# A wait that ties the first gathers of a graph-attention pass to the matmuls that use them

## Chip, cores and metric

One core of a Trainium2 chip runs the whole program. The metric is the device time of one execution in microseconds, and the median of several runs is compared. TensorE is PE in the rows, VectorE is DVE, ScalarE is ACT, GpSimd is POOL and SyncE is SP. Each is an instruction queue of its own, and they meet only at semaphores.

## What is computed

A small graph network on 3125 nodes of 256 features and 50000 edges, sorted by their target node:

```python
h   = relu(concat([x, segment_sum(edge_weight * x[dst], src)]) @ W + b)   # first layer
x   = layernorm(x + h)
y   = x
for Wl, Wr, att, b in two_layers:              # GATv2, 8 heads of 32 features, with self loops
    xl, xr = y @ Wl, y @ Wr
    e      = leaky_relu(xl[src] + xr[dst], 0.2)
    score  = sum(e * att, per head)
    alpha  = softmax of score over the edges of one dst
    y      = y + gelu(segment_sum(alpha * xl[src], dst) + b)
x   = layernorm(x + y)
```

The change lies in the loop over the edges of a GATv2 layer. It is built twice, once for each layer; these are called pass one and pass two here.

## The kernel before

The edges lie in blocks of 128, one edge to a partition, and G = 4 blocks make a group. A pass has NG = 110 groups, and K / G = 4 groups (WG) make a chunk. For each group q the following happens.

- **Gather** (POOL, L1058): four indirect DMAs fetch the rows of the edges' source nodes from a table in device memory (`gather_table`, 264 floats a row) into the ring `gath`. The ring holds RING = 12 groups. Each DMA is an instruction on POOL, which writes the descriptors, and lands some us later; `gathered[q % 12]` tells of it.
- **Expand** (PE, L1077 and L1081): four matmuls copy the gathered rows into PSUM, four more add the rows of the target nodes, picked by the one-hot matrix `OHT` that ACT makes (L1260, L1264). The trace shows eight and four pieces of them. The last adds one to `expanded`. There are two PSUM buffers, so `expand(q)` waits until DVE has read group q - 2.
- **Score** (DVE, L1136 and L1146): the leaky relu times the attention vector, and its sum by head.
- **Chunk** (PE, DVE, ACT): after the scores of four groups the running maximum by target node is found with scans and transposes, and the exponents are taken (ACT L1292, L1293), which adds to `exps`.
- **Weigh**: POOL multiplies half of the gathered rows by their exponents (L1015, `by_pool`), DVE the other half (also L1015, `by_dve`).
- **Sum** (PE, L1108): one-hot matmuls add up the weighted rows by target node (`summed`), and DVE adds the result to the accumulator `node` (L1190). For the first group of a chunk it first multiplies the accumulator by a growth factor (L1197, L1198).

PE works in steps t: `expand(t + 1)`, then what the chunk needs, then the sums of group t - LAG, with LAG = 6. So expansion 7 is followed by the sums of group 0, these by expansion 8, and these by the sums of group 1. POOL has one loop in one queue:

```python
for q in range(NG + RING - 2):
    a = q - RING + 2
    if a >= 0:
        pool.wait_ge(exps, 2 * (a // WG) + 2)
        weigh(pool, a, 0, 2, slots(a, 0, 2)[:, :, D:XW]).then_inc(by_pool, 1)
    if q < NG:
        gather(q)
```

So POOL gathers the groups 0 to 9 without a weighing between them, and from then on weighs group q - 10 and gathers group q. A gather of group 12 or later waits until the sums of the group that held its slot of the ring are done. The gathers of groups 0 to 11 fill the ring and wait for nothing.

Before the passes there are a stage that sorts and prepares, one that scatters weighted rows (POOL L670, with ACT L648 ahead of it), one that sums them and one that makes the table; behind each pass there is a short stage that joins the self loops.

Of the kernel before, what the change touches and what calls it, by code (L numbers as in the profile page):

```python
# [71 lines left out]
def build(nc, x, src, dst, edge_weight, W0, b0, gat, out):  # L72
# [46 lines left out]
    with top:  # L119
# [821 lines left out]
        for layer, (_, _, _, bias) in enumerate(gat):  # L941

            ctx, sem, ps = stage()
            with ctx:
# [27 lines left out]
                def by_head(a):  # L972
# [6 lines left out]
                hot_t, expanded, lin_ready, weighted, scored = (  # L979
                    sem("hot_t"), sem("expanded"), sem("lin_ready"), sem("weighted"), sem("scored"))  # L980
# [28 lines left out]
                def slots(q, g0, g1):  # L1009
                    i = G * (q % RING)  # L1010
                    return ROWS[:, i + g0:i + g1, :]

                def weigh(eng, q, g0, g1, by):
                    R = slots(q, g0, g1)[:, :, 0:D].rearrange("p g (h c) -> p g h c", h=H)
                    return eng.tensor_tensor(R, R, by.unsqueeze(3).broadcast_to([P, g1 - g0, H, C]), ALU.mult)  # L1015

                with nc.Block() as block:
# [32 lines left out]
                    @block.gpsimd  # L1050
                    def _(pool):
                        def gather(q):
                            if q >= RING:
                                pool.wait_ge(summed, 2 * (q - RING + 1))
                            pool.nop(nofuse=True)
                            for g in range(G):
                                i = G * q + g
                                pool.indirect_dma_start(ROWS[:, i % (RING * G), 0:XW], None, tab_d[:, :],  # L1058
                                                        bass.IndirectOffsetOnAxis(SRCI[:, i:i + 1], 0)).then_inc(gathered[q % RING], 16)
# [8 lines that stand above are left out]
# [601 lines left out]
```

## Time and profile before

| | |
|---|---|
| median of 3 runs | 2588.24 us (2587.32 to 2589.81) |
| profiled execution | 2584.12 us, span 2582.3 us |
| mean granted TensorE clock | 0.92 of full |
| busy: PE, DVE, ACT, POOL | 2086.6, 1593.4, 1056.8, 1662.7 us |
| pass one: first gather to last sums | 1033.3 to 1731.3 us |
| pass two: first gather to last sums | 1817.3 to 2514.7 us |

All times of rows are microseconds from the start of the span unless marked ns. A PE clock of 1.00 is the 2.4 GHz level, 0.50 the 1.2 GHz level. A row of a timeline can hold several instructions (its count stands behind the x), and then its duration is from the first one's start to the last one's end. Busy time doesn't count waits, branches and the issue of a DMA by SP.

### The profile page before, as it was taken

To read this page: it belongs to the slowest core of one execution; us is meant where nothing else is said; L and a number is where in the kernel's file an instruction comes from. 1 tells how busy PE (TensorE), PEld (TensorE's weight loads), DVE (VectorE), ACT (ScalarE), POOL (GpSimd) and SP (SyncE) were. 2 spreads that over 40 slices of the span, in tenths; PEclk is the share of its full clock that TensorE was granted. 3 is DMA by queue.
4 is the path that set the end of the run, shared out by engine and by line. 5 is a ranking of instruction groups with operands and counts; after the bars stand their busy time and mean duration, and the time that the engine had idled before them with its cause. 6 is when DMAs were issued, how large, how long until landed. Compare 5 with 4: busy or idle time off the path is not lost. (4 is left out here: it accounts for less than half of the span.)

```text
span 2582.3 us, 31699 instructions
## 1 busy us (share of the span) xinstructions
PE 2086.6 (81%) x7770; PEld 1439.5 (56%) x7770; DVE 1593.4 (62%) x3202; ACT 1056.8 (41%) x2798; POOL 1662.7 (64%) x1810
## 2 busy tenths in 40 slices
PE   0656666665499989799999999969699999999975
PEld 0444444444377765466666666645466666666654
DVE  8312111111266666488888888877488888888876
ACT  0233333333000013355555555544355555555543
POOL 3377777777400004788888888836788888888832
PEclk9776778778799999899999999989899999999987
DMA  3355353434499842544444444431444444444443
GB/s 95 83 123 118 120 117 120 114 119 118 124 267 265 264 126 77 132 113 112 113 126 111 112 113 113 108 65 47 123 110 114 112 115 113 114 111 112 113 78 100
DMA packets 208623, 311.81 MB, mean 121 GB/s; under 512 B 33396, under 2 KB 167542, under 8 KB 208471
## 3 DMA queue, kind: packets, MB, share of 16 engines
q0 software_dynamic: 64512, 171.82, 24.7%
q1 hardware_dynamic: 143799, 138.05, 21.1%
q8 instruction: 61, 1.00, 0.2%
q14 instruction: 91, 0.75, 0.1%
q10 hardware_dynamic: 160, 0.20, 0.0%
HBM read 243.75 MB, written 72.66 MB: 123 GB/s over the span
## 5 line engine op out<-in xcount | busy, mean ns | idle before, releaser
L1058 POOL DMA_INDIRECT gath<-gather_table,SRCI x880 | 849.0, 965 | 242.4 <-issue 210.4
L1108 PE MATMUL p_sums<-gath,OH 128*128 128x272 f32 x1760 | 476.6, 410 | 63.2 <-DVE gath L1015 29.1
L670 POOL DMA_INDIRECT rows_by_src<-gath,node x440 | 436.7, 993 | 139.7 <-issue 115.8
L615 PE MATMUL p_expd<-X,OHT 128*128 x880 | 301.6, 504 | 220.6 <-DVE OHT L581 220.5
L1077 PE MATMUL p_expd<-gath,ident 128*128 128x512 f32 x880 | 427.5, 609 | 31.9 <-DMA gath<-gather_table,SRCI 31.5
L1108 PEld LDWEIGHTS p_sums<-gath,OH 128*128 128x128 f32 x1760 | 323.2, 193 | 189.7 <-issue 86.6
L1081 PE MATMUL p_expd<-node,OHT 128*128 x1760 | 417.6, 380 | 0.0
L1081 PEld LDWEIGHTS p_expd<-node,OHT 128*128 128x128 f32 x1760 | 336.4, 191 | 142.0 <-issue 107.4
L615 PEld LDWEIGHTS p_expd<-X,OHT 128*128 128x128 f32 x880 | 210.6, 250 | 300.9 <-issue 264.1
L1136 DVE SCALAR_TENSOR_TENSOR work<-p_expd,VEC 128x512 f32<-128x512 f32 x440 | 282.2, 682 | 136.8 <-PE p_expd L1081 135.8
L648 ACT ACTIVATE gath<-p_expd,node 128x256 f32<-128x256 f32 x440 | 172.7, 476 | 387.7 <-DVE gath L584 336.8
L584 DVE CAST gath<-SRCI 128x4 f32<-128x4 int32 x110 | 24.1, 219 | 457.5 <-DMA rows_by_src<-gath,node 457.5
L1277 ACT ACTIVATE OH<-iota_row,NLOC 128x128 f32<-128x128 f32 x880 | 277.6, 385 | 6.3 <-PE p_sums L1108 6.2
L1146 DVE TENSOR_REDUCE scores<-work 128x32 f32<-128x1056 f32 x220 | 274.6, 1248 | 5.7
L1015 POOL TENSOR_TENSOR gath<-gath 128x512 f32<-128x512 f32 x220 | 232.2, 1058 | 60.3 <-ACT gath L1293 56.8
L748 PE MATMUL p_sums<-gath,OH 128*128 128x256 f32 x976 | 229.7, 389 | 44.5 <-DVE OH L721 43.4
L1077 PEld LDWEIGHTS p_expd<-gath,ident 128*128 128x128 f32 x880 | 160.0, 192 | 157.5 <-issue 108.2
L1260 ACT ACTIVATE OHT<-LBC,minus_p 128x512 f32<-128x512 bf16 x220 | 157.3, 715 | 209.3 <-PE p_expd L1081 209.3
L748 PEld LDWEIGHTS p_sums<-gath,OH 128*128 128x128 f32 x976 | 180.2, 191 | 94.4 <-DVE OH L721 36.6
L810 POOL TENSOR_TENSOR gath<-gath 128x256 f32<-128x256 f32 x25 | 18.3, 731 | 310.4 <-ACT gath L832 310.4
L1190 DVE TENSOR_TENSOR node<-node,p_sums 128x272 f32 x440 | 187.6, 426 | 17.3 <-PE p_sums L1108 15.9
L1282 ACT ACTIVATE OH<-OH,ones 128x512 f32<-128x512 f32 x220 | 155.6, 707 | 0.5
(282 smaller groups left out, 2163.0 us busy)
## 6 DMA issues: line engine op xcount, KB each, us to landing
gath<-rows_by_src SPq DMA_DIRECT2D x122, 514.0 KB, 4.5
LBC<-local_rows SPq DMA_DIRECT2D x330, 128.0 KB, 3.1
gath<-gather_table,SRCI POOLq DMA_INDIRECT x880, 3.0
rows_by_src<-gath,node POOLq DMA_INDIRECT x440, 3.5
gather_table<-gath SPq DMA_DIRECT2D x50, 132.0 KB, 1.7
node<-gather_table SPq DMA_DIRECT2D x2, 3200.0 KB, 11.9
X<-in_x SPq DMA_DIRECT2D x1, 3072.0 KB
x<-X SPq DMA_DIRECT2D x5, 512.0 KB, 3.0
```

What stands on the lines that cost most here:

```text
L615: ins = pe.matmul(expd[q % 2][:, g // 2, (g % 2) * D:(g % 2 + 1) * D], OHT[:, q % 2, g * P:(g + 1) * P], Xv[:, bass.ds(tiles[g // 2], 1), ...
L670: pool.indirect_dma_start(sup_d[:, :], bass.IndirectOffsetOnAxis(POSI[:, i:i + 1], 0), U[:, q % 4, g, :], None, bounds_check=EP - 1, oob_i ...
L748: ins = pe.matmul(sums[s][:, 0:D], OH[:, s % 2, g, :], U[:, s, g, 0:D], start=(g == 0), stop=(g == G - 1))
L1015: return eng.tensor_tensor(R, R, by.unsqueeze(3).broadcast_to([P, g1 - g0, H, C]), ALU.mult)
L1058: pool.indirect_dma_start(ROWS[:, i % (RING * G), 0:XW], None, tab_d[:, :], bass.IndirectOffsetOnAxis(SRCI[:, i:i + 1], 0)).then_inc(gathe ...
L1077: pe.matmul(expd[q % 2][:, k, :].rearrange("p (g n) -> p g n", g=2), ident[:, :], slots(q, 2 * k, 2 * k + 2)[:, :, 0:D], start=True, stop= ...
L1081: ins = pe.matmul(expd[q % 2][:, g // 2, (g % 2) * D:(g % 2 + 1) * D], OHT[:, q % 2, g * P:(g + 1) * P], TARGET[:, bass.ds(tiles[g // 2], ...
L1108: ins = pe.matmul(sums[k][:, 0:RW], OH[:, a % 2, g, :], slots(a, g, g + 1)[:, 0, :], start=(g % 2 == 0), stop=(g % 2 == 1))
L1136: ins = dve.scalar_tensor_tensor(Tv[:, q % 2, 2 * k:2 * k + 2, :, 0:C].rearrange("p g h c -> p g h c"), expd[q % 2][:, k, :].rearrange("p ...
L1146: dve.tensor_reduce(SC[:, q // WG % 2, :, k:k + G].rearrange("p h k -> p k h"), Tv[:, q % 2], AX, ALU.add).then_inc(scored, 1)
L1190: dve.tensor_tensor(ACC[:, bass.ds(j, 1), :], ACC[:, bass.ds(j, 1), :], sums[k][:, 0:RW].unsqueeze(1), ALU.add).then_inc(added, 1)
L1277: ins = act.activation(OH[:, a % 2, g, :], iota_row[:, :], ACT.Abs, bias=NLOC[:, i:i + 1])
```

## The change

While the ring fills, the gather of group q waits until `expanded` has reached q - 2, that is, until PE has expanded the groups 0 to q - 3. It holds for the groups 3 to 11 of both passes. `expanded` existed before, and ACT, DVE and SP wait for it already.

```diff
 def gather(q):
     if q >= RING:
         pool.wait_ge(summed, 2 * (q - RING + 1))
+    elif q >= 3:
+        pool.wait_ge(expanded, q - 2)
     pool.nop(nofuse=True)
     for g in range(G):
         i = G * q + g
```

## Rows read from the trace of the kernel before

**Rows 1.** The page, costliest groups: busy, mean ns | idle before, releaser

```profile
L1058 POOL DMA_INDIRECT gath<-gather_table,SRCI x880 | 849.0, 965 | 242.4 <-issue 210.4
```

**Rows 2.** Windows: length, busy time by engine, granted PE clock, DMA share, GB/s

```profile
core 0: us, PE busy (x) PEld busy (x) DVE busy (x) ACT busy (x) POOL busy (x), PEclk, DMA share, GB/s
1085.20:1088.60 3.40, 3.40 (x9) 2.19 (x8) 1.47 (x3) 0.00 (x0) 2.49 (x4) 0.50 0.38 107
1867.00:1873.60 6.60, 5.14 (x10) 3.53 (x11) 2.05 (x4) 1.62 (x4) 5.48 (x7) 0.50 0.44 124
...
1108.00:1685.00 577.00, 555.17 (x2112) 373.67 (x2111) 479.67 (x889) 334.72 (x888) 472.34 (x481) 1.00 0.46 113
```

**Rows 3.** Timeline of POOL, pass one: start, duration, instruction, idle before it

```profile
1083.26 1.05 POOL L1015 TENSOR_TENSOR gath<-gath 128x512 f32<-128x512 f32 x1
...
1089.23 1.05 POOL L1015 TENSOR_TENSOR gath<-gath 128x512 f32<-128x512 f32 x1
1090.44 0.98 POOL L1058 DMA_INDIRECT gath<-gather_table,SRCI  x1 [0.16 <-issue]
...
1095.19 1.06 POOL L1015 TENSOR_TENSOR gath<-gath 128x512 f32<-128x512 f32 x1
```

**Rows 4.** Timeline of PE around the first sums, pass one, then pass two

```profile
1074.73 1.99 PE L1081 MATMUL p_expd<-node,OHT 128*128 x8
...
1084.56 3.38 PE L1108 MATMUL p_sums<-gath,OH 128*128 128x272 f32 x8 [4.28 <-POOL gath L1015]
...
1089.88 1.89 PE L1081 MATMUL p_expd<-node,OHT 128*128 x8
...
1097.21 1.08 PE L1108 MATMUL p_sums<-gath,OH 128*128 128x272 f32 x4
...
1858.47 2.65 PE L1081 MATMUL p_expd<-node,OHT 128*128 x8
...
1868.46 3.97 PE L1108 MATMUL p_sums<-gath,OH 128*128 128x272 f32 x8 [3.79 <-POOL gath L1015]
...
1874.65 1.89 PE L1081 MATMUL p_expd<-node,OHT 128*128 x8
```

**Rows 5.** Timeline of POOL, pass two: group 9, group 11, end of gathers

```profile
1862.43 0.95 POOL L1058 DMA_INDIRECT gath<-gather_table,SRCI  x1 [0.30 <-issue]
...
1867.15 1.05 POOL L1015 TENSOR_TENSOR gath<-gath 128x512 f32<-128x512 f32 x1
...
1874.34 0.98 POOL L1058 DMA_INDIRECT gath<-gather_table,SRCI  x1 [0.16 <-issue]
...
2468.43 4.06 POOL L1015 TENSOR_TENSOR gath<-gath 128x512 f32<-128x512 f32 x4
```

**Rows 6.** Timeline of all engines: first scatter, and begin of pass one

```profile
105.33 1.20 ACT L648 ACTIVATE gath<-p_expd,node 128x256 f32<-128x256 f32 x3
...
107.49 1.03 POOL L670 DMA_INDIRECT rows_by_src<-gath,node  x1 [19.35 <-ACT gath L648]
...
1032.56 2.99 SPq L1043 DMA_DIRECT2D LBC<-local_rows  x4
1033.28 1.02 POOL L1058 DMA_INDIRECT gath<-gather_table,SRCI  x1 [2.51 <-POOLq L108]
```

**Rows 7.** Timelines near the end of pass one: POOL and PE

```profile
1673.02 1.06 POOL L1015 TENSOR_TENSOR gath<-gath 128x512 f32<-128x512 f32 x1
...
1674.29 1.16 PE L1108 MATMUL p_sums<-gath,OH 128*128 128x272 f32 x4
...
1684.95 4.05 POOL L1015 TENSOR_TENSOR gath<-gath 128x512 f32<-128x512 f32 x4
1706.49 4.07 POOL L1015 TENSOR_TENSOR gath<-gath 128x512 f32<-128x512 f32 x4 [17.49 <-ACT gath L1293]
```

**Rows 8.** Timelines: DVE's growth factor beside the first gather of a group

```profile
1132.17 0.43 DVE L1197 TENSOR_TENSOR node<-node,grow 128x256 f32 x1 [0.21 <-DVE node L1190]
1132.26 1.20 POOL L1058 DMA_INDIRECT gath<-gather_table,SRCI  x1 [0.16 <-issue]
...
1964.09 1.19 POOL L1058 DMA_INDIRECT gath<-gather_table,SRCI  x1 [0.16 <-issue]
```

## Prediction

> **What bounds the kernel now.** Read the page first, then the two passes alone, since only they hold the changed lines. The costliest group of the page is POOL's indirect gather, 880 instructions of 0.965 us, and nearly all the idle time before them (210.4 of 242.4 us) is "issue", the 0.3 us between two descriptors; it waits for others next to nothing [rows 1]. The windows of pass one say that PE is busy 555.2 of 577 us from 1108 to 1685 at full clock, so by busy share PE looks like the bound [rows 2]. The timeline of POOL decides it. A group costs POOL one weighing (1.05 us) and four gathers, 5.97 us from weighing to weighing (1083.26, 1089.23, then 1095.19 us) [rows 3]. The first weighing of pass one is at 1083.26 and the row that holds the one a hundred groups later starts at 1684.95 us [rows 3, 7]: 601.7 us, against 100 x 5.97 = 597. The other 4.7 us are dealt with below. In pass two it is 2468.43 - 1867.15 = 601.3 us [rows 5]. So POOL never waits between its first gather and its last; it runs on a timetable of its own, and PE follows it. At the end of pass one PE's sums of group 98 start at 1674.29 us, 0.21 us after POOL's weighing of that group ends (1673.02 + 1.06) [rows 7]. A POOL that is late by d there makes PE late by d. PE has little play, yet it has some: it is the follower.
>
> **The change part by part.** Nothing is removed and no data moves elsewhere. Nine waits are added in each of the two passes, ahead of the gathers of groups 3 to 11. Group q waits until PE has expanded group q - 3. From group 12 on the old wait stands as it was.
>
> Groups 3 to 9 come with four gathers at 1.25 us, 5.0 us a group, from 1033.28 us on, so group q starts at about 1033.3 + 5.0q [rows 6]; PE expands them about one group behind. The tightest of these is group 9 of pass two. It starts at 1862.43 us and needs expansion 6, which ends at 1858.47 + 2.65 = 1861.12 us [rows 4, 5]: 1.3 us of play, and more for the others (group 9 of pass one: about 1078.3 by the same count, against an expansion 6 that ends at 1074.73 + 1.99 = 1076.72). Group 10 needs expansion 7, done before PE goes idle for POOL's first weighing. These eight waits find their count reached and cost nothing; what hides them is the gather still running on POOL while its queue reads the wait.
>
> Group 11 is different, because here POOL waits for work that waited for POOL. Expansion 8 stands behind the sums of group 0 in PE's queue, and those wait 4.28 us for POOL's weighing of group 0, which is queued behind the gathers of group 9 [rows 3, 4]. The sums start at 1084.56; after them expansion 8 ends at 1089.88 + 1.89 = 1091.77 us. The gather of group 11 started at 1090.44 us. It is held 1.33 us. In pass two expansion 8 ends at 1874.65 + 1.89 = 1876.54 us and the gather started at 1874.34: 2.20 us [rows 4, 5]. Behind the waiting instruction stand the four gathers of group 11, the weighing of group 2 and all later groups of the same queue.
>
> To this comes the way from the release to the first descriptor, with POOL's pipe empty. No wait of the passes shows it, since none of them holds POOL today. Two places are near. In the scatter stage ACT's fourth scaling ends at 106.53 and the first scatter starts at 107.49 us: 0.97 us. After the barrier at the start of pass one SP's first transfer starts at 1032.56 and POOL's first gather at 1033.28 us: 0.7 us, a lower bound, since SP needs something too [rows 6]. I take 0.9, as the first is the same kind of wait and the same kind of instruction; the bounds are 0.6 and 1.0. The Trainium skill, "Advanced Engine Details and Errata", section Network/Comms, gives 50 to 100 ns for a sequencer to read a semaphore; if that were all, the stall would be 1.33 + 0.1 and 2.20 + 0.1, 3.7 us in total. The row with 0.97 us speaks against it.
>
> The stall is then 1.33 + 0.9 = 2.23 us and 2.20 + 0.9 = 3.10 us, 5.33 us together. The first gather after an empty pipe takes 1.02 us instead of 0.98 [rows 3, 6]: 0.1 us for both passes.
>
> Is it caught up? PE has play right behind the stall: sums of group 2 start at 1097.21 and their weighing ended at 1096.25 us, 0.96 us earlier [rows 3, 4]. But this only means that PE falls into step with POOL some groups sooner. POOL has no idle time in which to win back a microsecond, and the last sums hang on POOL [rows 7]. After 1685 POOL waits 17.49 us for ACT's exponents, which hang on PE, so the drain starts late by the same amount.
>
> One small term is left, the 4.7 us from above. Some first gathers take 1.20 instead of 0.98 us, those that run beside DVE's multiplication of the sums by the growth factor, once in four groups (1132.17 DVE, 1132.26 POOL) [rows 8]. 4.7 / 0.2 is 23 of these in pass one, 4.3 / 0.2 is 21 in pass two. They come from 1132 us on in pass one and regularly from 1964 us on in pass two [rows 8], that is, once PE and DVE are in step with POOL. With the stall they are in step sooner: one more in pass one, two in pass two, 0.6 us. Bounds: none, and five (1.0 us). The Trainium skill, "SBUF — State Buffer", section Terms, says that DVE and GpSimd hold a shared port exclusively and the loser blocks for the whole instruction; by it a gather would lose up to 0.43 us, and these rows show 0.2.
>
> Sum: 5.33 + 0.1 + 0.6 = 6.0 us. The profiled execution of 2584.12 us (span 2582.3) would become 2590.1 (span 2588.3). The median of the runs is 4.1 us above that execution; I carry the difference over, 2588.24 + 6.0 = **2594.2 us**, +0.23%. About 0.2% (5.2 us) is what a measurement of this kernel can tell from no change, so the forecast lies just past that line.
>
> What moves the sum most is PE's clock while it does sums 0 and expansion 8, just after its idle. In pass one 3.4 us of them ran at 0.50 (the level of 1.2 GHz), in pass two 5.1 us, from 1868.46 to 1873.6, of a stretch that began before them [rows 2, 4]. Work at half speed loses half its time: 1.7 and 2.6 us. All at full speed the stalls would be 2.23 - 1.7 = 0.5 and 3.10 - 2.6 = 0.5 us, 1.0 together; with 3.4 us more at half speed in each they would be 8.7. Idle of 4.28 us came before the fall both times, so I expect it again, and take 3.0 to 8.5 us as bounds.
>
> **The rivals.**
> *The same stall, but below the line.* Mechanism as above, with less of the half-speed clock or a release of 0.6 us: 1.9 + 2.8 = 4.7 us, or 3 us with a shorter slow stretch, 2591 to 2593. It is the low half of the forecast, and "no change" by measurement.
> *A second stall at group 9.* Expansion 6 also ran partly at half speed (2.65 instead of 1.89 us for its second half) [rows 4]. With 3.4 us more of that it ends 1.7 us later, and the 1.3 us of play less the 0.9 of the release are used up: 1.3 us of stall in pass two, 0.8 in pass one. All behind it moves too, the weighing of group 0 included, so it adds to the stall of group 11: +7 to +8.5 us, 2596. For it: the play is just 0.4 us net. Against it: both passes of this execution keep it.
> *The wait does nothing.* If POOL's queue had the gathers of group 11 dispatched before the count matters, or if PE's backlog covered it: 2588.2. Against it: the gather of group 11 starts before expansion 8 ends in both passes, and the wait stands ahead of it.
> *Faster.* The 44 long first gathers cost 9 us. A stall that shifts POOL against DVE for good would free them: -9 + 5.4, 2584.7 us. It decides from 27 avoided on (5.4 / 0.2). Against it: both passes began with another distance between PE and POOL and both ended in the same step, so the distance is not kept.
>
> **How the numbers follow.** Stall at group 11 alone, passed on whole: 0.77, of it 0.46 past the line and 0.31 below it. Second stall: 0.12, nearly all past the line. No effect: 0.07. Faster: 0.04, half of it by over 0.2%. Slower by over 0.2%: 0.46 + 0.11 = 0.57. Within: 0.41. Faster: 0.02. The range takes the clock's bounds of 3.0 and 8.5 us and 1 us of scatter between runs (2587.32 to 2589.81): 2590.2 to 2597.8.
>
> **What would show it.** POOL idle once per pass before the first gather of group 11, 2 to 3 us, released by an expansion of PE; no idle before groups 3 to 10; the weighings after it again 5.97 us apart; the last gather of each pass late by the stall; PE waiting for the weighing of group 2. Idle of 0.2 us there would refute the release time; a last gather that is not late would refute that POOL sets the pace; expansion 8 without a half-speed stretch would make the forecast too high.

## The result: slower by 0.29%, and the profile after

| | before | changed |
|---|---|---|
| median of 7 runs | 2587.32 us (2584.63 to 2589.81) | 2594.91 us (2591.12 to 2598.44) |
| profiled execution | 2584.12 us, span 2582.3 | 2591.98 us, span 2590.2 |

The ratio is 1.0029, with a 95% interval of 1.0019 to 1.0038: 5 to 10 us slower. Other chips on which the kernel before takes about 2586 us agree with it as far as they were tried (experiments 1 to 4). Two more chips take 2724 and 2735 us for the kernel before. On the second of them the same change made it faster by 1%, and on the first the waits ahead of groups 3 to 10 alone did; experiment 7 is about that.

POOL's timeline of the changed kernel (start, duration, instruction, idle before it), around group 11 of pass one and of pass two, and at the last gathers of each:

```profile
1088.91 1.06 POOL L1015 TENSOR_TENSOR gath<-gath 128x512 f32<-128x512 f32 x1
1092.93 0.98 POOL L1060 DMA_INDIRECT gath<-gather_table,SRCI  x1 [2.96 <-PE p_expd L1083]
...
1097.70 1.05 POOL L1015 TENSOR_TENSOR gath<-gath 128x512 f32<-128x512 f32 x1
...
1687.89 4.05 POOL L1015 TENSOR_TENSOR gath<-gath 128x512 f32<-128x512 f32 x4
...
1879.29 1.06 POOL L1015 TENSOR_TENSOR gath<-gath 128x512 f32<-128x512 f32 x1
1882.37 0.98 POOL L1060 DMA_INDIRECT gath<-gather_table,SRCI  x1 [2.02 <-PE p_expd L1083]
...
2477.13 2.06 POOL L1015 TENSOR_TENSOR gath<-gath 128x512 f32<-128x512 f32 x2
```

Between the weighing of group 1 and the first gather of group 11 there were 0.16 us of idle [rows 3]; now there are 2.96 and 2.02 us, and PE's expansion ends them. That is 2.80 + 1.86 = 4.66 us more. PE's timeline at the same places:

```profile
1084.25 3.96 PE L1110 MATMUL p_sums<-gath,OH 128*128 128x272 f32 x8 [4.28 <-POOL gath L1015]
...
1090.29 1.89 PE L1083 MATMUL p_expd<-node,OHT 128*128 x8
...
1098.96 2.07 PE L1110 MATMUL p_sums<-gath,OH 128*128 128x272 f32 x8 [1.18 <-issue]
...
1874.63 3.54 PE L1110 MATMUL p_sums<-gath,OH 128*128 128x272 f32 x8 [5.29 <-POOL gath L1015]
...
1879.72 1.89 PE L1083 MATMUL p_expd<-node,OHT 128*128 x8
```

Expansion 8 ends at 1090.29 + 1.89 = 1092.18 us and the gather of group 11 starts at 1092.93: the release takes 0.75 us. In pass two it is 1881.61 to 1882.37, 0.76 us. (In the source an expansion is two matmuls at L1079 and four at L1083; the trace shows them as four and eight pieces.) PE now waits 1.18 us before the sums of group 2 start, 0.21 us after their weighing ends (1097.70 + 1.05 = 1098.75); before, they had 0.96 us of play [rows 3, 4].

The idle of POOL ahead of all 880 gathers of the changed kernel, by what ended it:

```profile
L1060 POOL DMA_INDIRECT gath<-gather_table,SRCI x880: 942/949/1231, 1032.8 to 2476.2; - x176
its engine sat idle before it (us, times) until:
  issue: 208.8, 780
  PE p_sums L1110: 28.7, 94
  PE p_expd L1083: 5.6, 4
  POOLq L108: 4.0, 2
```

The four events by an expansion are the two stalls and two ordinary gaps of 0.3 us behind an early release. From the first gather to the weighing of group 100 it was 1684.95 - 1033.28 = 651.67 us in pass one before [rows 6, 7] and is 1687.89 - 1032.83 = 655.06 now, 3.39 more. In pass two, whose first gather was at 1817.33 us and is at 1823.46, 651.10 became 653.67, 2.57 more. Together 5.96 us. The spans differ by 7.9 us: 3.2 us more lie between the two stretches, and what stands before the first and behind the second is 1.3 us shorter.

### The profile page after: what moved, and what is told of

It reads as the page before. It is cut to its first block and busy times, and to the rows that moved or that the text cites. A ratio compares the mean times of both kernels' runs of the same rounds, so it can differ in the third digit from the quotient of the medians.

```text
span 2590.2 us, 31717 instructions
## 1 busy us (share of the span) xinstructions
PE 2083.3 (80%) x7770; PEld 1438.5 (56%) x7770; DVE 1596.0 (62%) x3202; ACT 1056.7 (41%) x2798; POOL 1663.2 (64%) x1810
## 5 line engine op out<-in xcount | busy, mean ns | idle before, releaser
L1079 PE MATMUL p_expd<-gath,ident 128*128 128x512 f32 x880 | 424.9, 606 | 32.5 <-DMA gath<-gather_table,SRCI 31.9
L1083 PE MATMUL p_expd<-node,OHT 128*128 x1760 | 417.5, 380 | 0.0
L1083 PEld LDWEIGHTS p_expd<-node,OHT 128*128 128x128 f32 x1760 | 336.1, 191 | 141.3 <-issue 106.7
L1079 PEld LDWEIGHTS p_expd<-gath,ident 128*128 128x128 f32 x880 | 159.2, 192 | 157.1 <-issue 107.1
```

Source lines behind the costliest of these rows:

```text
L1079: pe.matmul(expd[q % 2][:, k, :].rearrange("p (g n) -> p g n", g=2), ident[:, :], slots(q, 2 * k, 2 * k + 2)[:, :, 0:D], start=True, stop= ...
L1083: ins = pe.matmul(expd[q % 2][:, g // 2, (g % 2) * D:(g % 2 + 1) * D], OHT[:, q % 2, g * P:(g + 1) * P], TARGET[:, bass.ds(tiles[g // 2], ...
```

## The experiments

Two theories stood at first. **A**: POOL sets the pace of a pass, the wait holds it once in each, and what it is held comes out at the end. **B**: the other eight waits cost something too. Further rivals are named with their run. The runs went to several chips; each is compared with the kernel before on its own chip. All line numbers of the changed kernel are two higher behind the new lines.

**1. Group 11 alone.**

```diff
-    elif q >= 3:
+    elif q == RING - 1:
         pool.wait_ge(expanded, q - 2)
```

> The new wait is kept ahead of the gather of group 11 alone; groups 3 to 10 have none. Theory A (one stall per pass, at group 11, passed on to the end): as with all nine waits, +6 us over the kernel before (+4.5 to +8), POOL idle for 2 to 3 us ahead of group 11 in each pass. Theory B (the eight other waits cost something too, as instructions in POOL's queue or by holding back its reading ahead): clearly less than with all nine, +3 us or below.

2590.91 us against 2584.92, ratio 1.0026 (1.0016 to 1.0035). POOL is idle 2.08 and 2.05 us ahead of group 11. On another chip of the same speed it was run again beside the kernel before itself.

> The wait ahead of group 11 alone. Chip like the first: +6 us over the kernel before, as measured there. Chip like the second, theory E (the gain of 28 us there comes from the waits ahead of groups 4, 8 and 9, which hold POOL's gathers back so that the small loads land): these waits are gone, so the gain is gone, the fill takes 70 us or more again, and the time is 0 to +8 us over the kernel before. Theory F (the gain comes from group 11): most of the 28 us stay.

2594.59 us against 2586.77, ratio 1.0027 (1.0016 to 1.0039), with idle of 2.27 and 3.05 us. One wait of nine makes the whole loss.

> The kernel before itself, for a profile from the same chip as the runs beside it. Ratio 1.000. On a chip like the first (some 2585 us): ring filled to the first weighing in 50 us, 6.02 us a group after it. On a chip like the second (some 2735 us), theory E: ACT's first step of the one-hot matrix waits 20 us or more for its small load in the fill of the ring, since POOL's free-running gathers stand ahead of that load in the DMA engines, and the first weighing comes 70 us or more after the first gather.

Its ratio was 1.000 (0.9989 to 1.0011). In this execution the stretch from first gather to weighing 100 took 652.8 and 652.4 us, against 651.7 and 651.1 in the one shown: about 1 us of a pass is scatter between executions of one kernel.

**2. All but group 11.**

```diff
-    elif q >= 3:
+    elif 3 <= q < RING - 1:
         pool.wait_ge(expanded, q - 2)
```

> The new waits stand ahead of groups 3 to 10, and group 11 has none. Theory A: no change against the kernel before, within 2.5 us, and no idle of POOL above 0.31 us between the gathers of groups 0 to 9. Theory B: +2 us or more.

2584.08 us against 2584.92, ratio 1.0000 (0.9992 to 1.0009), and no idle of POOL above 0.31 us in the fill. Theory B falls.

**3. A longer stall in the same place.**

```diff
-    elif q >= 3:
-        pool.wait_ge(expanded, q - 2)
+    elif q == RING - 1:
+        pool.wait_ge(expanded, q - 1)
```

> Only group 11 waits, and for expansion 9 in place of 8. Expansion 9 ended at 1097.16 and 1881.93 us in the kernel before, the gather of group 11 began at 1090.44 and 1874.34. Theory A, with the 0.76 us that the release took in the changed kernel's trace: stalls of 7.5 and 8.4 us, so +16 us over the kernel before (+14 to +19), and +10 over the change. Theory C (PE has play, and what is lost early is won back over the hundred groups that follow, so a longer stall costs hardly more): +6 to +9 us.

2600.28 us, ratio 1.0064 (1.0050 to 1.0077), so 13 to 20 us, middle 16.5. POOL's timeline at group 11 of pass one and pass two:

```profile
1087.56 1.06 POOL L1015 TENSOR_TENSOR gath<-gath 128x512 f32<-128x512 f32 x1
1096.92 0.98 POOL L1060 DMA_INDIRECT gath<-gather_table,SRCI  x1 [8.29 <-PE p_expd L1083]
...
1888.68 0.98 POOL L1060 DMA_INDIRECT gath<-gather_table,SRCI  x1 [8.40 <-PE p_expd L1083]
```

The idle beyond the usual 0.16 us is 8.13 + 8.24 = 16.4 us, and the loss is as long. Nothing is won back over a hundred groups.

**4. PE kept busy before the first sums.** The change with all its waits, and

```diff
+if t == LAG:
+    for _ in range(4):
+        pe.matmul(sums[1][:, :].rearrange("p (g n) -> p g n", g=2),
+                  ident[:, :], TARGET[:, 0:2, :], start=True, stop=True)
 for a in sums_at(t):
     pe.wait_ge(hots, a + 1)
```

> The change with all its nine waits, and four extra matmuls of 128x512 into the still unused second PSUM buffer of the sums, once a pass, just ahead of the sums of group 0, where PE is idle for some 4 us. They compute nothing that is used. If the half-speed clock on sums 0 and expansion 8 makes most of the stall, expansion 8 now ends 1 to 2 us sooner in each pass, POOL is held 0.6 to 1.5 us in place of 1.9 and 2.8, and the time is +2 to +4 us over the kernel before. If the clock doesn't answer to these matmuls, the stalls stay and the time is that of the change, +6 to +7.

2585.36 us against 2584.92, ratio 1.0006 (0.9998 to 1.0015), so -0.5 to +3.9 us. PE's timeline in pass one, and its windows in both passes (the column behind the busy times is the granted clock):

```profile
1082.35 3.60 PE L1103 MATMUL p_sums<-node,ident 128*128 128x512 f32 x8
1086.79 2.07 PE L1113 MATMUL p_sums<-gath,OH 128*128 128x272 f32 x8 [0.85 <-POOL gath L1015]
1088.70 1.88 PE L1079 MATMUL p_expd<-gath,ident 128*128 128x512 f32 x4
1090.42 1.89 PE L1083 MATMUL p_expd<-node,OHT 128*128 x8
```

```profile
core 0: us, PE busy (x) PEld busy (x) DVE busy (x) ACT busy (x) POOL busy (x), PEclk, DMA share, GB/s
1085.00:1092.00 7.00, 6.15 (x23) 3.83 (x21) 1.83 (x4) 1.46 (x4) 5.88 (x7) 1.00 0.41 119
1870.00:1877.00 7.00, 6.83 (x24) 3.98 (x22) 2.19 (x4) 1.85 (x5) 5.89 (x7) 1.00 0.48 127
```

The same stretches of the changed kernel without the extra matmuls:

```profile
1085.00:1092.00 7.00, 7.00 (x20) 4.72 (x19) 1.47 (x3) 0.00 (x0) 4.04 (x5) 0.71 0.32 87
1874.00:1882.00 8.00, 7.37 (x23) 5.36 (x24) 1.83 (x4) 0.29 (x1) 5.26 (x6) 0.79 0.35 93
```

With the gap filled the clock stayed at 1.00 (2.4 GHz). Without, it was 0.71 and 0.79 on average, that is, partly at 0.50. The sums took 2.07 us in place of 3.96 and 3.54, expansion 8 ended 5.5 us after their start in place of 7.9 and 7.0, and POOL was idle for 0.56 us in each pass, 0.4 more than usual. From the first gather to the weighing of group 100 it was 651.87 and 651.48 us, 0.2 and 0.4 more than in the kernel before. So with all nine waits in place nearly all of the loss of these stretches is gone, more than the expectation had it (+2 to +4 us), and most of the stall is PE at half speed after its own idle. A run with the extra matmuls and no waits is missing.

**5 and 6. POOL made faster.** POOL weighs one block of a group and DVE three, without the new waits and with them.

```diff
-weigh(pool, a, 0, 2, slots(a, 0, 2)[:, :, D:XW])
+weigh(pool, a, 0, 1, slots(a, 0, 1)[:, :, D:XW])
...
-weigh(dve, a, 2, G, ... EXPS[:, G * (a % WG) + 2:G * (a % WG) + G, :])
+weigh(dve, a, 1, G, ... EXPS[:, G * (a % WG) + 1:G * (a % WG) + G, :])
```

The first try came to one of the other chips.

> The kernel before, without the new waits, but POOL weighs one of the four blocks of a group and DVE three, in place of two and two. Theory A (POOL's timetable sets the pace of a pass): a group costs POOL 5.97 - 0.5 = 5.5 us, below the 5.8 us (23.1 us for four groups) that PE needed in pass one before it fell into step, so the pace goes to PE: 6.02 to about 5.8 or 5.9 us a group, 12 to 22 us a pass, 25 to 45 us in all. Theory D (PE or DVE sets the pace, and POOL only seems to): no gain, or a loss, since DVE has 0.3 us more work a group.

> The same division of the weighing with all nine new waits. Theory A: POOL has time in hand once PE sets the pace, so the stall at group 11 (about 2.5 us a pass) costs only what of it reaches PE at the sums of group 2, less than 1 us a pass: 0 to +2.5 us over the kernel with the same division and no waits. The rival, that a stall of POOL costs its length whoever sets the pace: +5 to +6 us.

There they took 3152.56 and 3108.76 us, against 2734.84 for the kernel before: 15% and 14% slower. A group took 8.07 us after the fill, in place of 6.02. Nothing in theory A had foreseen it; what these traces show of the fill is told below. On a chip like the first both were run again.

> No new waits, POOL weighs one block of four and DVE three. Chip like the first, theory A: 12 to 22 us less a pass, 25 to 45 us less in all, as expected before. Theory D: no gain or a loss. Chip like the second: some 3150 us again.

> The same division with the nine waits. Chip like the first: 0 to +2.5 us over the kernel with the same division and no waits (theory A), against +5 to +6 if a stall of POOL costs its length whoever sets the pace. Chip like the second: some 3110 us again, 40 us less than without the waits.

2540.45 us without and 2538.57 us with the waits (four runs each), against 2586.77: ratios 0.9818 (0.9802 to 0.9834) and 0.9810 (0.9793 to 0.9826). The gain of 46 us lies just above the 25 to 45 expected. Windows without the waits, in pass one after the fill:

```profile
1110.00:1630.00 520.00, 508.30 (x1984) 353.16 (x1984) 453.68 (x831) 313.50 (x830) 404.81 (x451) 1.00 0.47 119
```

PE is busy 98% of it, against 96% before [rows 2], and a hundred groups take 576.2 in place of 601.7 us. POOL's queue at group 11 with the waits:

```profile
1091.86 0.63 POOL L1015 TENSOR_TENSOR gath<-gath 128x256 f32<-128x256 f32 x1
1095.16 0.99 POOL L1060 DMA_INDIRECT gath<-gather_table,SRCI  x1 [2.67 <-PE p_expd L1083]
```

The stall is still there, an idle of 2.67 us in pass one and 0.98 us in pass two, and costs nothing that can be measured: from the first gather to the weighing of group 100 it took 626.5 and 624.9 us with the waits and 626.1 in both passes without them. Where POOL doesn't set the pace, its stall is free. This confirms theory A from its other side, and it is the fastest version found: 1.8% below the kernel before on such chips.

**7. The change on another chip.**

> The changed kernel itself, beside the others on one chip: +6 to +8 us over the kernel before (ratio 1.0023 to 1.0031), POOL idle 2 to 3 us ahead of the gather of group 11.

It came to the same chip as the first try of 5 and 6: 2707.26 us against 2734.84, ratio 0.9904 (0.9880 to 0.9929). Faster, against the expectation. That made theory **E**: transfers land later on such a chip, and POOL's gathers, running free in the fill, stand in the way of the small loads of local rows (`LBC`, on SP's queue) that ACT needs to make the one-hot matrices. The early waits hold the gathers back. The rival **F** was that the gain comes from group 11. The last run, on a third chip that takes 2723.71 us for the kernel before, tells them apart.

> The waits ahead of groups 3 to 10 alone, once more, since the calls fall on different chips. Chip like the first: no change against the kernel before, within 2.5 us. Chip like the second (the kernel before at some 2735 us), theory E: these waits hold the whole gain, some 28 us less than the kernel before, first weighing about 60 us after the first gather in each pass; theory F (it comes from group 11): 0 to -5 us.

2696.83 us, ratio 0.9899 (0.9879 to 0.9919), so -27 us with the waits ahead of groups 3 to 10 alone. F falls, as far as two chips can be compared; group 11 alone was not run on such a chip. Nor is there a trace of the kernel before from one: its place is taken by the first try of experiment 5, whose fill up to the first weighing has the same program. ACT's timeline in the fill of pass one, first that kernel without waits, then this last run:

```profile
1144.97 0.72 ACT L1260 ACTIVATE OHT<-LBC,minus_p 128x512 f32<-128x512 bf16 x1 [2.76 <-issue]
...
1161.65 0.72 ACT L1260 ACTIVATE OHT<-LBC,minus_p 128x512 f32<-128x512 bf16 x1 [15.20 <-issue]
...
1188.37 0.72 ACT L1260 ACTIVATE OHT<-LBC,minus_p 128x512 f32<-128x512 bf16 x1 [25.24 <-DMA gather_table<-gath]
```

```profile
1139.69 0.72 ACT L1262 ACTIVATE OHT<-LBC,minus_p 128x512 f32<-128x512 bf16 x1 [2.97 <-issue]
...
1149.58 0.72 ACT L1262 ACTIVATE OHT<-LBC,minus_p 128x512 f32<-128x512 bf16 x1 [8.18 <-PE p_expd L1083]
...
1156.42 0.72 ACT L1262 ACTIVATE OHT<-LBC,minus_p 128x512 f32<-128x512 bf16 x1 [3.39 <-issue]
```

Without waits ACT stands 15.2 and 25.2 us before this one instruction, which needs two things: the load of local rows, and the count `expanded`, which tells that the buffer is free. Theory E says that it is the load. PE's and DVE's timelines of the same kernel say that it is the count:

```profile
1147.34 1.89 PE L1081 MATMUL p_expd<-node,OHT 128*128 x8
...
1151.87 1.89 PE L1081 MATMUL p_expd<-node,OHT 128*128 x8
```

```profile
1144.91 1.29 DVE L1136 SCALAR_TENSOR_TENSOR work<-p_expd,VEC 128x512 f32<-128x512 f32 x2 [11.54 <-issue]
...
1161.59 1.29 DVE L1136 SCALAR_TENSOR_TENSOR work<-p_expd,VEC 128x512 f32<-128x512 f32 x2 [14.10 <-issue]
...
1188.31 1.29 DVE L1136 SCALAR_TENSOR_TENSOR work<-p_expd,VEC 128x512 f32<-128x512 f32 x2 [24.14 <-DMA gather_table<-gath]
```

This step of DVE needs the expansion of its group and no load of local rows. Yet DVE stood until the same moments as ACT, which followed 0.06 us behind it each time. Expansions 1 and 2 ended by PE's rows at 1149.23 and 1153.76 us, so their counts reached both engines 12.4 and 34.6 us late. The load, as far as the trace has it, came long before. SP's queue tells when the loads of groups 3 (the last of the first row) and 4 (the first of the second) were issued:

```profile
1131.88 1.75 SPq L1043 DMA_DIRECT2D LBC<-local_rows  x4
...
1140.88 22.60 SPq L1043 DMA_DIRECT2D LBC<-local_rows  x4
```

A load lands in sixteen parts, and the trace has only some of them: six of group 3, landed from 1136.0 to 1137.3 us, and three of group 4, from 1144.0 to 1144.7, all within 5 us of the issue.

In the run with the waits POOL waits for the same count ahead of group 4. PE's expansion 1, and DVE and POOL:

```profile
1142.40 1.89 PE L1083 MATMUL p_expd<-node,OHT 128*128 x8
```

```profile
1149.52 1.29 DVE L1138 SCALAR_TENSOR_TENSOR work<-p_expd,VEC 128x512 f32<-128x512 f32 x2 [7.32 <-PE p_expd L1083]
```

```profile
1150.24 0.94 POOL L1060 DMA_INDIRECT gath<-gather_table,SRCI  x1 [3.35 <-PE p_expd L1083]
```

Expansion 1 ended at 1144.29 us. ACT, DVE and POOL (less the 0.76 us of its release) all went on at 1149.5, 5.2 us later. The trace records the counts of expansions 1 and 2 at 1149.49 and 1149.62 us, 0.13 apart, though the matmuls of an expansion take 3.7 us. So the signal was late and not the work. Ahead of group 8 it is the same (expansion 5 ended at 1166.04, counted at 1172.74). Group 9 waits for expansion 6, which itself ended late, at 1180.8, behind these. On the chips of 2586 us DVE starts 0.04 us after the end of each of the first five expansions. Theory E is thus wrong in what it says is late.

POOL's first gather and first weighing, the same two kernels:

```profile
1132.61 1.02 POOL L1058 DMA_INDIRECT gath<-gather_table,SRCI  x1 [3.23 <-POOLq L108]
...
1206.85 0.62 POOL L1015 TENSOR_TENSOR gath<-gath 128x256 f32<-128x256 f32 x1 [24.44 <-ACT gath L1293]
```

```profile
1127.06 1.02 POOL L1060 DMA_INDIRECT gath<-gather_table,SRCI  x1 [2.51 <-POOLq L108]
...
1173.48 0.95 POOL L1060 DMA_INDIRECT gath<-gather_table,SRCI  x1 [3.53 <-DMA gather_table<-gath]
...
1181.54 0.95 POOL L1060 DMA_INDIRECT gath<-gather_table,SRCI  x1 [3.29 <-PE p_expd L1083]
...
1186.27 1.06 POOL L1015 TENSOR_TENSOR gath<-gath 128x512 f32<-128x512 f32 x1
```

The fill takes 74.2 us without waits and 59.2 us with them; in pass two 77.2 and 59.5. The first tries of 5 and 6, which differ by the waits alone and ran on one chip, have 74.2 and 77.2 against 59.5 and 59.8: 32 us of the 44 by which their medians differ. On the chips of 2586 us the fill takes 50 us either way.

Why the counts are late is argued and not shown. In the three traces from such chips that have waits, the late counts ahead of groups 4 and 8 came 2.6 to 3.1 us after POOL's last gather before the wait had ended, twelve times of twelve, and elsewhere a gather lands in 3.0 us in the middle. That fits gathers in flight that hold the signal up and let it through once they have landed, so that a held POOL would free it. No run takes the two apart.

The 8.07 us a group of the other division look like the same thing. Once in four groups DVE's scan at L1152 started 3.3 us (in the middle) after the end of the PE transposition it waits for, and the one at L1161 4.6 us after its own; with the same division on a chip of 2586 us it was 0.04 and 0.09 us. Together that is 7.8 us, where four groups took 9.2 us longer. L1161 also needs a load whose landing isn't recorded.

## Why the prediction was right, and where not

**Who sets the pace** was right, and experiments 3 and 5 to 6 show it from both sides: a longer stall costs its whole length, and with a faster POOL a stall costs nothing. By busy share alone PE would have been named.

**Eight free waits** were right where the profile had been taken (experiment 2), and wrong on two chips, where the waits of groups 4, 8 and 9 hold POOL for over 3 us each and, with the others up to group 10, make the gain.

**The stall at group 11** was forecast as 2.23 and 3.10 us and was 2.80 and 1.86; the sum, 5.33 against 4.66, is 0.7 too high. Of it 0.3 us are the release, taken as 0.9 and measured as 0.76. The rest is the end of expansion 8, which hangs on how much of the half-speed stretch falls on it: 2.04 and 1.10 us behind the gather's old place, in place of 1.33 and 2.20. That 5.33 came so near was partly luck: one pass came out 0.6 us over and the other 1.2 under. The 50 to 100 ns of the Trainium skill ("Advanced Engine Details and Errata", Network/Comms) are a part of the 0.76 at most.

**The clock as the largest unknown** was right: without the half-speed stretch the two stalls are 0.4 us each (experiment 4), where the prediction worked out 0.5. The idle before it was 4.28 us in pass one alone and 3.79 in pass two [rows 4], not 4.28 both times.

**The term that failed** is that of the long first gathers. They were to become three more, 0.6 us. Counted by their durations, the changed kernel has 23 and 22 of them, against 23 and 21: one more, 0.2 us. PE and DVE did come into step sooner, but the first long one of pass one still belongs to group 18.

**The second stall at group 9** did not come in any run on a chip like the first. On the two others it did, as a consequence of PE's late signals and not by the clock.

**The sum** of 6.0 us agrees with 5.96 in the profiled execution and with 5 to 10 us over the runs, though partly by luck: the stalls make 4.7, and the 1.3 us left in these stretches are no larger than the scatter between executions. In the runs of experiment 1 the stalls were 3.8 and 5.0 us and the medians 6 to 8 us higher. One to three microseconds of the loss are not assigned; the stretch from the weighing of group 100 to the last sums took 45.9 to 48.4 us in six passes with the wait and 45.2 to 47.5 us in six without it, which is too few to tell a difference from scatter.

**What no rival covered** is a gain by the early waits. The one on the faster side was about DVE and POOL in step. In the trace of before DVE starts 0.04 us behind the end of the first five expansions, so nothing in it pointed there.

Left open is why PE's signals reach the other engines late on two of the chips, and why they do so in the middle of a pass with the other division of the weighing only. The traces from these chips lack part of their records of signals and landings, and whether that has the same cause isn't known.

## What to carry to other kernels

Find the engine that never waits before costing a wait; a microsecond of it is a microsecond of the kernel, and one of any other engine may be free. When a wait is put on that engine, look whether the work waited for is itself queued behind that engine's own output: here it was, after an idle that also halved PE's clock. When an engine stands still, look at a second engine that waits for the same signal before blaming what only the first needs: here that told a late count from a late load. Run a change to when transfers start on more than one chip: this one is -1% or +0.3% by the chip, and the division that gains 1.8% on one kind loses 15% on the other.

## What was not expected of the hardware

- POOL started its first descriptor 0.75 to 0.77 us after the end of the matmul it waited for, in all six stalls at group 11 in the changed kernel and in experiments 3 and 4.
- Four otherwise useless matmuls, 3.6 us of work in a 4.3 us gap, kept PE at 2.4 GHz through the next sums in both passes (granted clock 1.00 in place of 0.71 and 0.79), and with that took away most of the loss.
- On two of the four chips of the experiments counts by PE's matmuls reached DVE, ACT and POOL 5 to 7 us late in the fill with the waits, and 12 to 36 us late without them, against 0.04 us on the others.
- These two chips run the same kernel 5 to 6% slower, with 6.02 us a group and PE's granted clock at 1.00 in the middle of a pass (in the changed kernel and in the last run of experiment 7). Those two runs lose time in the scatter stage, some 93 us, and in the fill of the ring. The first gather of pass one comes at 1127 us in them, against 1033.
